# Eight places instead of four for the gathered expert rows of the second mixture layer

## The reference

```python
x = x + tanh(g_xattn[0]) * L0_xattn(layernorm(x), ctx, ...)
x = x + tanh(g_ffn[0])   * L0_ffn(layernorm(x), ...)     # 8 experts, the 2 best of each token
x = x + tanh(g_xattn[1]) * L1_xattn(layernorm(x), ctx, ...)
x = x + tanh(g_ffn[1])   * L1_ffn(layernorm(x), ...)     # 16 experts, the 4 best of each token

def L1_ffn(x):
    probs = softmax(x @ router_w.T); vals, idx = top_k(probs, 4)
    w_dense = zeros.at[token, idx].set(vals)
    for e in range(16):                       # intermediate width 176
        h = silu(x @ gate_w[e].T) * (x @ up_w[e].T)
        acc += w_dense[:, e, None] * (h @ down_w[e].T)
    shared = silu(x @ shared_gate_w.T) * (x @ shared_up_w.T) @ shared_down_w.T   # width 704
    return acc + sigmoid(x @ se_gate_w.T) * shared
```

## Time and profile before

| part of the page | value |
|---|---|
| PE busy | 848.2 us, 80% of the span |
| DVE busy | 746.2 us, 71% |
| POOL busy | 628.4 us, 59% |
| ACT busy | 472.7 us, 45% |
| chain that ended last, by engine | PE 40%, DVE 16%, POOL 13%, issue 12% |
| POOL DMA_INDIRECT L736 into sb_stg, x32 | 31.8 us busy, 40.2 us idle before |
| ACT L850, x48 | 28.6 us busy, 158.4 us idle before |

### The profile page before, as it was taken

The page is one execution under the profiler, slowest core; times in us unless marked ns, Lnnn a source line. Parts: engine busy times, 40 slices in busy tenths (PEclk is TensorE's granted clock), DMA queues, the critical chain, the costliest instruction groups (busy, mean ns, idle before and its releaser), DMA issues.

```text
span 1058.2 us, 21126 instructions
## 1 busy us (share of the span) xinstructions
PE 848.2 (80%) x6928; PEld 577.9 (55%) x6929; DVE 746.2 (71%) x1571; ACT 472.7 (45%) x1018; POOL 628.4 (59%) x830
## 2 busy tenths in 40 slices
PE   4489668699898878888888788858689999869756
PEld 2257545477655545555555455544568888645333
DVE  5778767566567688898798788947757777545545
ACT  3445244233222458767667667834034344312111
POOL 4586881666275868878778788710144444534551
PEclk9689959799999956686687677858789999979788
DMA  7021242244332231121110100010034444432322
GB/s 254 21 83 29 58 132 65 72 147 146 117 104 69 75 133 37 65 94 46 61 42 15 29 26 4 2 64 23 11 95 141 136 132 140 131 105 85 96 79 70
DMA packets 65766, 85.55 MB, mean 81 GB/s; under 512 B 11148, under 2 KB 56976, under 8 KB 65680
## 3 DMA queue, kind: packets, MB, share of 16 engines
q1 hardware_dynamic: 55312, 55.30, 16.2%
q0 software_dynamic: 10368, 29.14, 10.4%
HBM read 61.93 MB, written 32.98 MB: 90 GB/s over the span
## 4 chain that ended last, share of the span: by engine, by line
PE 40%; DVE 16%; POOL 13%; issue 12%; POOLq 5%; ACT 4%; DVEq 4%; DMA 2%; another core or an unknown queue 2%; SPq 1%; ACTq 0%
PE PS L261 24%; DVE sb_slotv L1403 5%; PE PS L768 4%; POOL sb_xnf L702 3%; DVE sb_wkh L1408 2%; PE PS L792 2%; PE PS L821 2%; PE PS L1284 2%; PE PS L370 1%; PE PS L1274 1%; PE PS L397 1%; PE PS L268 1%; POOL sb_region L1512 1%; POOL sb_xnf L736 1%
## 5 line engine op out<-in xcount | busy, mean ns | idle before, releaser
L261 PE MATMUL PS<-sb_region,sb_wkh 88*128 (+1 forms) x1440 | 213.5, 300 | 12.5 <-DVE sb_wa L976 10.5
L702 POOL DMA_INDIRECT sb_xnf<-token_table,sb_ids x120 | 116.2, 968 | 172.9 <-DVE sb_ids L613 83.5
L1403 DVE TENSOR_REDUCE sb_slotv<-PS 128x1 f32<-128x512 f32 x256 | 163.7, 682 | 26.0 <-PE PS L1274 25.9
L261 PEld LDWEIGHTS PS<-sb_region,sb_wkh 88*128 88x128 f16 (+1 forms) x1440 | 142.3, 100 | 61.3 <-issue 17.7
L261 PE MATMUL PS<-sb_xnT,sb_sgu 128*128 128x512 f16 x528 | 130.0, 398 | 5.7 <-issue 5.0
L768 PE MATMUL PS<-sb_sdn,sb_wkh 128*128 128x256 f16 (+1 forms) x576 | 75.5, 281 | 33.2 <-DVE sb_wkh L936 20.4
L850 ACT ACTIVATE sb_wk<-PS 128x512 f32<-128x512 f32 (+1 forms) x48 | 28.6, 596 | 158.4 <-PE PS L261 113.5
L1358 ACT ACTIVATE sb_wk<-PS,sb_slotv 128x512 f32<-128x512 f32 x128 | 87.1, 689 | 23.5 <-DVE sb_slotv L1403 23.2
L261 PEld LDWEIGHTS PS<-sb_xnT,sb_sgu 128*128 128x128 f16 x528 | 52.5, 101 | 68.9 <-issue 19.6
L1742 POOL TENSOR_SCALAR sb_wk<-sb_wk 128x512 f32<-128x512 f32 x128 | 79.8, 623 | 16.2 <-ACT sb_wk L1358 6.8
L768 PEld LDWEIGHTS PS<-sb_sdn,sb_wkh 128*128 128x128 f16 (+1 forms) x576 | 55.6, 100 | 55.8 <-DVE sb_wkh L936 26.1
(11 more groups left out here) (305 smaller groups left out, 1884.5 us busy)
## 6 DMA issues: line engine op xcount, KB each, us to landing
slot_table<-sb_wa SPq DMA_DIRECT2D x60, 256.0 KB
slot_table<-token_table SPq DMA_DIRECT2D x16, 640.0 KB
sb_stg<-gu SPq DMA_DIRECT2D x24, 352.0 KB, 3.0
sb_stg<-dn SPq DMA_DIRECT2D x24, 176.0 KB
token_table<-sb_xnf SPq DMA_DIRECT2D x16, 256.0 KB, 3.9
sb_stg<-sgu SPq DMA_DIRECT2D x8, 352.0 KB, 6.9
sb_x_sb<-x SPq DMA_DIRECT2D x1, 2048.0 KB, 12.1
out<-sb_x_sb SPq DMA_DIRECT2D x16, 128.0 KB
```

Of the source, the lines that this page charges most:

```text
L261: last = nc.tensor.matmul(out_, lhs(i, c), rhs(j, c), start=(c == 0 and n == 0 and not begun), stop=(c == C - 1 and n == 2 and not more))
L702: nc.gpsimd.indirect_dma_start(xg[l][:, 2 * (g % XR) + n, :], None, xw[l][:, :], bass.IndirectOffsetOnAxis(ap=ids[:, 2 * g + n:2 * g + n + ...
L1403: nc.vector.tensor_reduce(h_nb[u][:, h:h + 1], PS[:, 2 * u + h, :], AX, ALU.max, negate=True).then_inc(h_max, 1)
```

## The change

```diff
@@ -323,10 +323,10 @@
-        CR = (4, 4)
+        CR = (4, 8)
@@
-        c_ld = list(zip(*(both(f"c_ld{r}", 16 * TOPK[0] * len(range(r, NT, CR[0]))) for r in range(max(CR)))))
+        c_ld = list(zip(*(both(f"c_ld{r}", 16 * TOPK[0] * len(range(r, NT, CR[0])) * (r < CR[0])) for r in range(max(CR)))))
@@ -341,7 +341,11 @@
         rows_at = ([xnf_flat[:, r * 2 * D:(r + 1) * 2 * D] for r in range(CR[0])],
-                   [stg_flat[:, 0:4 * D], stg_flat[:, 4 * D:8 * D], wqp32, xnf_flat[:, 12 * D:16 * D]])
+                   [stg_flat[:, 0:4 * D], stg_flat[:, 4 * D:8 * D], wqp32, xnf_flat[:, 12 * D:16 * D]]
+                   + [reg32[:, 4 * D * r:4 * D * (r + 1)] for r in range(4)])
+        experts_over = -(-4 * 4 * D // (2 * EG))
+        assert (T * TOPK[1] + (P - 1) * experts_over) // P <= NS[1] - 2 * XR, \
+            "the last groups, those whose x rows are still to be taken when all are fetched, are of none of the first experts"
```

## The result

| | us |
|---|---|
| before, median of 4 runs on this chip | 1066.99 (1064.95 to 1070.78) |
| changed, median of 4 | 1080.93 (1071.22 to 1085.15) |
| ratio | 1.0119, 95% interval 1.0067 to 1.0171 |
| changed, profiled execution (span) | 1077.57 (1075.8) |

The change made the kernel slower by 1.2% on this chip. On another chip, as the experiments show, it makes it faster by 1%. So the document has two halves: the trace here, which follows the forecast in its order but costs more than it, and what it was that the forecast took for a property of the kernel.

A forecast was written before the change was run, and what follows sets the result against it. The prediction took the end to be bound by PE, starved while gathers follow without a break. +13.4 + 2.0 - 9.5 = +5.9 us on the median 1067.05 gave 1073.0 us, own range 1068 to 1078, 8-in-10 range 1054 to 1081.

The forecast's parts named there:

- Part 1: First burst, 24 gathers in place of 12: PE comes back 14.7 us later, less 1.3 for creeping; +13.4 us.
- The creeping: PE's slow issue during the longer first burst, one matmul in 1.4 us, worth 1.3 us at full pace.
- Part 2: Expert-15 gathers, 8 in place of 4 over the experts' last groups: +2.0 us, ends 0 to +7.0.
- Part 3: Bursts in the shared steps: second burst 12 gathers instead of 16, last burst gone; -9.5 us.
- The slower rival: Eight expert-15 gathers also stop the experts' last groups, shared steps start only behind: +12.2, 1079.3 us; chance 0.13.
- First rival: PE's stop in the first burst ends by itself near 934, so part 1 is 0: 1057.5 us; chance 0.22.
- Second rival: Gathers don't cause PE's stops; places bound, all PE idle time after 951 goes: -27.4, 1039.7 us; chance 0.08.
- Third rival: PE waits for its own instructions, stops at fixed program places: about 1067 us; chance 0.15 with other no-effect cases.
- The rule on POOL's descriptors: GpSimd's DMA descriptors are made by software in one queue, so more places make no gather quicker; 1.26 us each.
- the four coincidences of burst and stop: Before, in four long gather bursts from 918 us on, PE or its news stopped, returning 1.1 to 3.3 us after.

The follow-up runs named there:

- none2: Kernel before without the second layer's 64 expert-row gathers, on a chip with stops: 1012.68 us beside 1062.75, one run.
- e2_none: Kernel before without the second layer's 64 expert-row gathers, on a chip without stops: 1010.44 us beside 1021.86, ratio 0.9900.
- after2: The changed kernel again, unaltered, on another chip with stops: 1074.81 us beside 1062.75 for the kernel before, ratio 1.0121.
- order2: Eight places with the kernel before's gather order up to expert 15, on a chip without stops: 1016.17 us beside 1026.67, ratio 0.9898.
- e1_order: Eight places with the kernel before's gather order up to expert 15, then 16 more gathers directly behind; chip without stops: 1012.13 us beside 1021.86, ratio 0.9895.
- after: The changed kernel's first profile, on a chip with stops: median 1080.93 us beside 1066.99 for the kernel before, ratio 1.0119.
- after3: The changed kernel, unaltered, on a chip without stops: 1013.30 us beside 1025.33 for the kernel before, ratio 0.9901.
- e4_pause: Kernel before with a POOL drain and three memsets behind each four second-layer gathers, chip without stops: 1073.34 us beside 1021.86, ratio 1.0508.

## Why the prediction was right, and where not

**Sign and mechanism: right on its chip; the size: over half of it missed.** The longer first burst and the second burst cost more than the shared steps give back. none2 shows by experiment that the gathers cause PE's stops there. Of the 50 us that they cost on such a chip, 11 are there without any stop too (e2_none); the other 39 go with the stops, an estimate across two chips. But the median of 1080.93 lies above the forecast's own range (1068 to 1078) and only 0.07 us inside the wide one (1054 to 1081): +13.9 us for a forecast of +5.9. And that the result came from a chip with stops was luck: on the other kind the same change is 1.0% faster.

**Part 1 (+13.4): +16.8 up to ACT's first gate-up behind the burst, +14.7 up to the second.** The added burst time was right, 15.0 for 14.7. PE came back 4.5 us behind the burst in place of 2.7, a loss of 1.8 that the sum had not. The creeping was slower than I took it, one matmul in 2.1 to 2.8 us for 1.4, but its gain is there: PE had issued seven of the next gate-up's 12 matmuls by 956.1, and so ACT's second L882 comes 1.6 us behind the first where before it was 3.8. That is 2.2 us for the 1.3 forecast.

**Part 2 (+2.0): +4.6, or +6.8 counted from that second gate-up.** This is the term that was most under-sized, near its upper end of 7.0. The value taken came from the stretch of the first layer that didn't stop PE. Here 3.9 us of it are no stop at all but the lower clock: 2.6 for the 24 matmuls from 959.57, which PE began 2.2 us before the first of the eight gathers, and 1.2 for the last 12. Beside the eight gathers there is a short stop too: the transposes that PE ends at 968.00 reach ACT at 971.70, 3.7 us late, where before it was 0.3.

**Part 3 (-9.5): -8.4.** 20 gathers and then 12, as forecast, and the third stop's end is 5.5 us nearer to its burst's start (17.4 for 22.9 us). The first 36 matmuls ran at the lower clock after the stop, 10.35 us for 7.93, which the sum had not: 2.4 us of loss; without it the part is -10.8. The last stop ended 34 us before the end, not 40; by the sum's own terms it should have been 35 (39.7 before, less 2.9 and 1.6).

The sum was +5.9 and came to +13.0, short by 7.1 us. Of these 6.3 are work behind a stop at the lower clock (2.6, 1.2 and 2.4). The sum priced that clock once, with 1.6 us for the burst that goes away, and let PE come back at full clock from the stop that had become longer.

**The slower rival (the second burst stops the experts too): nearest in the number, half right in the mechanism.** I gave it 0.13, with +14.7 + 7.0 - 9.5 and 1079.3 us. The terms came to +14.7, +6.8 and -8.4. But PE still issued its transposes at once when DVE was done, at 967.36 and 5.6 us into the burst of eight, and over half of the 6.8 is the clock, so the agreement is in part luck. The forecast and this rival differ above all in part 2 (2.0 and 7.0), and part 2 was nearer to the rival.

**First rival (the stop ends by itself): half seen, and refuted.** I had named as the sign of the forecast that ACT's next L869 comes near 949, behind the burst. It came at 937.85 (L873 in the kernel after), with 14.5 us of gathers still to come, as this rival says: 15.3 us behind the first gather, where before it was 15.9. So the 1.1 us between the burst's end and this signal before were chance; in after2 it came 8.7 us behind the first gather. The release of what PE had queued is slow and not tied to the burst's end. But nothing more came until 956.84, so the stop did not end, and part 1 was not 0.

**Second rival (places are the bound): wrong here, right elsewhere.** I gave it 0.08 and -27.4 us. On the chips without stops it is what happens, with -12.0 us (1013.30 for 1025.33). Its size was wrong because I read PE's idle time, of which the stops were the larger part.

**Third rival (PE's own instructions, stops at fixed places): refuted,** by none2 and by every run on the other chips, whose PE has the same program. Whether on such a chip the gathers hold up PE's instruction blocks is another question, which no run tests; in the profile after no instruction packet is moved from 942 to 962 us. That instruction blocks are fetched ahead and mostly hidden, as the Trainium skill has it in "Runtime: NRT & Kernel Launch", "Instruction fetch mechanics", agrees with them: PE is busy 83.45 of 86 us in order2.

**The rule on POOL's descriptors** (the Trainium skill, "DMA: Bandwidth & Descriptors", "SWDGE vs HWDGE vs iDMA") held, a gather takes 1.25 us everywhere, but it didn't speak against the change: POOL's 64 gathers fit beside PE's steps, and what before lost was POOL's waiting for places.

**What the forecast could not see** is that the four coincidences of burst and stop hold on one kind of chip only. The trace before had no sure sign of it. In the first layer PE is busy beside the gathers, but these come at most eight in a row there, and the four stops lie in runs of 12 to 20.

**What stays open:** what in such a chip makes gathers stop PE; whether it is the bytes, the descriptors or the count; whether the order of e1_order would have avoided the loss on such a chip, where it was not run, so that the longer first burst is read from two traces there (after, after2) and not tested; and whether shorter bursts help there. The traces with stops lean to yes, though no run tests it: beside four gathers in a row (from 940) and beside eight in the first layer nothing stops, and beside eight in the kernel after ACT is late by 3.7 us. Nothing here beats the changed kernel on a chip without stops by more than the interval (e1_order's order, 0.9895 and 0.9898, after3 0.9901), and on a chip with them only the changed kernel and the one without gathers were run beside the kernel before, so no complete kernel is known to beat it there.

## What to carry to other kernels

When a stall in a trace coincides with another engine's bursts, take the bursts out and run both on the same chip before you size a change by them: here that one run (none2) was worth more than all rows. Compare absolute times only within a chip: the same kernel took 1025 and 1063 us on two of them, and the same change was worth -1.0% and +1.2%. A buffer that lets a queue run further ahead also takes away the pauses in its bursts, and here the stop grew with the burst on one kind of chip; on the other kind it is a gain of 1%. And when a stop gets longer, price the work behind it at the lower clock: here that was 6.3 of the 7.1 us that the sum fell short.

## What the runs showed of the hardware

Beside 12 to 24 gathers that POOL issued without a pause, TensorE's results came late on one kind of chip, so that ACT waited up to 18.4 us (after) and 23.2 us (after2); beside 64 in a row over 84 us on another chip (order2) nothing came late, with the same program on PE. On the first kind PE's issue fell to one matmul in 1.4 to 2.8 us, and a finished step reached ACT up to 30.5 us behind the end that the profile gives (924.39 + 1.95 to 956.84 in after), while DVE, ACT and POOL kept their pace: a gather took 1.25 us on both. While PE issued so slowly the granted clock was 0.50 (942 to 952 us in after), and it was 0.50 still in the first 5 us of the shared steps (977 to 982). A drain of POOL behind four gathers left it idle for 2.0 to 2.7 us, and for 7.0 behind the first four (e4_pause).
